# Attention on one core: softmax sums on GpSimd, an image's norms on ScalarE, the first maxima from full-precision operands, filler matmuls, transposed maxima two slots later

## The reference

```python
x = _group_norm(input, gn_weight, gn_bias)                  # 16 groups of 8 channels
qkv = jnp.einsum('bchw,oc->bohw', x, qkv_weight)            # 4 heads of 32 channels: q, k, v
attn = jnp.einsum('bnchw,bncyx->bnhwyx', q, k) / math.sqrt(C)
attn = jax.nn.softmax(attn.reshape(B, N_HEAD, H, W, H * W), axis=-1)      # over 1024 keys
out = jnp.einsum('bnhwyx,bncyx->bnchw', attn, v).reshape(B, C, H, W)
x = jnp.einsum('bchw,oc->bohw', out, out_weight) + out_bias[:, None, None] + input
t = tokens(x)                                               # (B, 1024, 128)
t = t + linear_attention(_ln_t(t))                          # _ln_t: layer norm over the 128 channels
t = t + experts(_ln_t(t))                                   # its own norm, router, top 2 of 8 experts
```

## Time and profile before

| | us |
|---|---|
| median of 3 runs (391.53, 394.69, 396.52) | 394.69 |
| the profiled execution | 393.55 |
| its span in the profile | 391.8 |

### The profile page before, as it was taken

How to read it: one execution, slowest core, us unless ns; L and a number is a source line. 1 busy time by engine, 2 the same in 40 slices (tenths; PEclk the granted TensorE clock), 3 DMA queues, 4 the chain that set the end, 5 groups by cost and what they waited for, 6 DMA issues and landing times.

```text
span 391.8 us, 6547 instructions
## 1 busy us (share of the span) xinstructions
PE 326.7 (83%) x1970; PEld 208.4 (53%) x1970; DVE 222.2 (57%) x693; ACT 187.9 (48%) x272; POOL 112.0 (29%) x142
## 2 busy tenths in 40 slices
PE   1766739998989989999999878198865998999985
PEld 1433323333433433544524254197865998999985
DVE  2446823456464556264655865376978566888610
...
DMA packets 21773, 29.29 MB, mean 75 GB/s; under 512 B 4055, under 2 KB 15628, under 8 KB 21484
## 3 DMA queue, kind: packets, MB, share of 16 engines
...
## 4 chain that ended last, share of the span: by engine, by line
PE 57%; DVE 18%; DMA 7%; POOL 7%; issue 6%; SPq 2%; ACT 1%; ACTq 0%; DVEq 0%; POOLq 0%
PE ps L794 13%; PE ps L989 8%; PE ps L977 8%; PE ps L757 6%; POOL expert_in L473 6%; PE ps L775 5%; DVE above L1081 4%; PE ps L737 3%; DMA Qs<-mrow 2%; SPq L331 2%; DMA Qs<-q_hi 2%; DVE pm L1084 2%; DMA attn<-in_L_conv_qkv_weight 1%; PE ps L859 1%; PE ps L693 1%
## 5 line engine op out<-in xcount | busy, mean ns | idle before, releaser
L536 ACT ACTIVATE probs<-ps 128x1024 f32<-128x1024 f32 x64 | 65.3, 1022 | 43.4 <-PE ps L775 43.4
L794 PE MATMUL ps<-probs,vT 128*32 128x512 f32 x256 | 69.2, 617 | 0.1
L794 PE MATMUL ps<-probs,ones 128*32 128x512 f32 x256 | 69.2, 617 | 0.0
L1081 DVE CUSTOM_DVE_ANT_0 above<-ps,above 128x512 f32<-128x512 f32 x56 | 38.7, 691 | 50.3 <-PE ps L757 49.0
L416 POOL TENSOR_TENSOR rstd<-ve,minus_half 128x8 f32<-128x8 f32 (+1 forms) x8 | 11.1, 1385 | 191.5 <-DVE ve L1120 175.2
L989 PE MATMUL ps<-w,GT 128*128 x368 | 52.8, 289 | 7.9 <-ACT GT L637 7.3
L637 ACT ACTIVATE GT<-H 128x512 f32<-128x512 f32 x46 | 29.0, 631 | 57.4 <-DVE H L1342 57.2
L989 PEld LDWEIGHTS ps<-w,GT 128*128 128x128 f32 x368 | 48.0, 204 | 9.6 <-issue 9.5
L977 PE MATMUL ps<-XTT,w1s 128*128 128x128 f32 x368 | 52.4, 289 | 0.0
L529 ACT ACTIVATE above<-ps 128x512 f32<-128x512 f32 x56 | 33.5, 599 | 38.5 <-PE ps L737 38.5
L478 POOL DMA_INDIRECT token_out<-Y,yidx x46 | 44.1, 959 | 22.1 <-DVE Y L1353 14.3
...
## 6 DMA issues: line engine op xcount, KB each, us to landing
...
```

Of the source, the lines that this page charges most:

```text
L536: nc.scalar.activation(probs[:, s % 3, :], bank(2 + 2 * (s % 2), 2), ACT.Exp).then_inc(exp_done, 1)
L794: last = nc.tensor.matmul(bank(6 + o % 2)[i * HD:(i + 1) * HD, :], w, probs[:, s % 3, hd * HALF:(hd + 1) * HALF], start=kt == 0, stop=kt = ...
L1081: nc.vector.tensor_tensor_reduce(above[:, n % 2, :], bank(base), above[:, n % 2, :], scale=1.0, scalar=-3.0e38, op0=ALU.add, op1=ALU.max, ...
```

## The change

**Sums.** The ones leave `values`. It now has four matmuls of 256 columns: two halves `i` of the 512 queries by two heads, in the four column groups of a bank. POOL adds the probabilities of every four steps (a quad), 128x1024 f32, three adds a quad (one in the last), into one of three buffers (`add_probs`, `quad_sum`). Once in eight steps PE multiplies two such sums with ones (`sums_of`), at the second step of the next output; the last one takes two further tiles of probabilities instead of waiting for their adds. `probs` has five buffers (`probs_of`); an exponential waits for the adds of the step five before. The closing on DVE is one step later.

**Maxima.** The slots of k = 0 are computed by `max_tile` from f32 copies `q32` and `k32` (two more ACT passes) with 32 rows of a head: per query tile four f32 matmuls of 512 columns, two heads by two key halves, in three or four pairs of banks. They stand ahead of image 1's projections, which now wait for those banks, and need no stacks. The transposition of k = 0 stands right behind its eight slots, and ACT issues its DMA; for every other k it stands two slots later than before. The 3 MB of zeros wait for that DMA.

**Norms.** The token norms of image 0 (`F` twice) and the last norm of both images (`X2`) move from DVE to ACT: eight activations of 128x128 each with scale and bias, after DVE has made the shift from mean and factor (`first_shift`, `v_shift`). POOL's powers for image 0 stand between its adds (`NORMS_AT`: after the add of step 35, 50 and 54). The router's logits are taken of the tokens before the norm: the router's weights are centred once ("centre": one matmul and one DVE operation), and `v_gates` multiplies by the norm's factor. So "tokenT" needs `t2` alone. `row_numbers` of image 1 is written after the adds.

**Fillers.** `keep_busy` issues f32 matmuls on the identity into bank 5: 3 at the start, 1 before the weight transposes, 1 of 256 columns and 2 around the group statistics, and 4 ahead of the first transposed maxima.

```diff
+    NPR = 5
+    QUADS = UNITS * 2 * L // P // 4
+    QSPAN = 256
...
+        def probs_of(s):
+            r = s % NPR
+            if r < 3:
+                return probs[:, r, :]
+            return (probs_a if s < UNITS * STEPS // B else probs_b)[:, r - 3, :]
+
+        def quad_sum(q):
+            return (X[:, 1, :], t2[:, 1, :, :].rearrange("p j c -> p (j c)"),
+                    X2[:, 1, :, :].rearrange("p j c -> p (j c)")[:, 0:L])[q % 3]
...
-        order = [(k, i) for k in range(2 * UNITS) for i in range(RING - 1)]
-        for k in range(2 * UNITS):
-            order.insert(min(RING * (k + 1), len(order)), (k, "rows"))
+        order = [(0, QH * hd + t) for t in range(QH) for hd in range(2)]
+        order += [(k, i) for k in range(1, 2 * UNITS) for i in range(RING - 1)]
+        order.insert(PLAIN_FIRST, (0, "rows"))
+        for k in range(1, 2 * UNITS):
+            order.insert(min(RING * (k + 1) + 2, len(order)), (k, "rows"))
...
-            return (6, 7) if g < AHEAD and g % 2 else (0, 1)
+            if g < PLAIN_FIRST:
+                return ((4, 5), (2, 3), (6, 7), (0, 1))[g % 4]
+            return (6, 7) if g == PLAIN_FIRST else (0, 1)
...
-        LAYER1_AT = {BEGIN_LAYER1: "residual", 34: "project", 35: "tokens_stats tokens", 39: "keys",
-                     40: "keys_exp", 41: "query_value0", 42: "query_value1", 44: "keyT", 45: "queries_exp",
+        LAYER1_AT = {BEGIN_LAYER1: "centre residual", 35: "project", 36: "tokens_stats", 38: "tokens", 40: "keys",
+                     41: "keys_exp", 42: "query_value0", 43: "query_value1", 44: "keyT", 45: "queries_exp",
                      46: "queries queries_scaled context", 47: "fold", 48: "queryT", 49: "queryT_sb",
-                     50: "attend stats", 52: "norm stats2", 54: "tokenT", 55: "tokenT_sb", 56: "logits",
-                     57: "gates_exp", 58: "route choose", 60: "counts norm2"}
+                     50: "attend stats", 51: "tokenT", 52: "tokenT_sb norm", 53: "logits",
+                     54: "stats2 gates_exp", 55: "route choose", 56: "shift norm2", 57: "counts"}
         LAYER1_AT_TILE = {"before": "residual project tokens_stats tokens keys keys_exp query_value0 query_value1 "
                                     "keyT queries_exp",
                           0: "queries queries_scaled context", 1: "fold", 2: "queryT queryT_sb", 3: "attend stats",
-                          4: "norm", 5: "stats2 tokenT", 6: "tokenT_sb", 7: "logits", 8: "gates_exp",
-                          9: "route choose counts norm2"}
+                          4: "tokenT tokenT_sb norm", 5: "logits stats2", 6: "gates_exp", 7: "shift route choose norm2",
+                          8: "counts"}
...
-            pool.wait_ge(mhl_ready, 1)
+            pool.wait_ge(mrow_in[0], 16 * 2)
...
+            def add_probs(q, i):
+
+                s = 4 * q + i
+                pool.wait_ge(exp_done, s + 1)
+                if i == 1 and q >= 3:
+                    pool.wait_ge(sum_done, (q - 3) // 2 + 1)
+                if i > 1:
+                    pool.wait_ge(probs_added, added_by(s - 1))
+                nc.gpsimd.tensor_tensor(quad_sum(q), probs_of(s - 1) if i == 1 else quad_sum(q), probs_of(s),
+                                        ALU.add).then_inc(probs_added, 1)
+
+            pool.wait_ge(resid_ready, B)
+            for q in range(QUADS):
+                if q == 1:
+                    pool.wait_ge(xs_zeroed, 16 * B)
+                    row_numbers(0)
+                for i in range(1, 4 if q < QUADS - 1 else 2):
+                    add_probs(q, i)
+                    if (q, i) in NORMS_AT:
+                        rsqrt(B + NORMS_AT[q, i])
...
-                if s >= 3:
-                    act.wait_ge(pv_done, s - 2)
-                nc.scalar.activation(probs[:, s % 3, :], bank(2 + 2 * (s % 2), 2), ACT.Exp).then_inc(exp_done, 1)
+                if s == 3:
+                    act.wait_ge(stack_in[0], 16 * (6 + SP_LOADS))
+                    act.wait_ge(stack_in_pool, 16 * (6 - SP_LOADS))
+                    act.wait_ge(stack_in[1], 16 * 12)
+                if s >= NPR:
+                    act.wait_ge(pv_done, s - NPR + 1)
+                    act.wait_ge(probs_added, added_by(s - NPR))
+                nc.scalar.activation(probs_of(s), bank(2 + 2 * (s % 2), 2), ACT.Exp).then_inc(exp_done, 1)
...
+            def first_apply(i, done):
+
+                act.wait_ge(nm_ready, i + 1)
+                for j in range(J):
+                    last = nc.scalar.activation(F[:, j, :], t2[:, 0, j, :], ACT.Identity, bias=nm[:, i, j:j + 1],
+                                                scale=rstd[:, B + i, j:j + 1])
+                last.then_inc(done, 1)
...
+            act.wait_ge(mrow_ready, 1)
+            for hd in range(2):
+                dst = Qs[SPLIT:STACK, 0, head(0, hd), 0:HALF]
+                act.dma_start(dst.bitcast(f32).rearrange("s (t q) -> s t q", t=QH),
+                              mrow[hd * 2 * QH:(hd + 1) * 2 * QH, :].bitcast(f32)).then_inc(mrow_in[0], 16)
...
+            def keep_busy(n, at_, width=4):
+
+                for i in range(n):
+                    nc.tensor.matmul(bank(at_)[:, 0:width * P], ident[:, :],
+                                     ident[:, :].unsqueeze(1).broadcast_to([P, width, P]), start=True, stop=True)
...
+            def max_tile(t):
+
+                g = 2 * t
+                if t == 0:
+                    pe.wait_ge(hi_ready, 2)
+                    pe.wait_ge(qk_split, 1)
+                    pe.wait_ge(v_sb, 1)
+                elif t == 1:
+                    pe.wait_ge(qk_split, 2)
+                    pe.wait_ge(kd_made, 1)
+                    pe.wait_ge(wT_sb, 2)
+                    pe.wait_ge(vcol_sb, 2)
+                else:
+                    pe.wait_ge(slot_used, g - 2)
+                for h in range(2):
+                    for hd in range(2):
+                        r = slice(HD * head(0, hd), HD * head(0, hd) + HD)
+                        last = nc.tensor.matmul(bank(slot_banks(g + hd)[h]), q32[r, t * P:(t + 1) * P],
+                                                k32[r, h * HALF:(h + 1) * HALF], start=True, stop=True)
+                        if h:
+                            last.then_inc(slot_ready, 1)
...
-            def values(u, step, hd):
-                s = u * STEPS + step
-                b, qh, kt = u // PAIRS, step // KT, step % KT
-                o = 2 * u + qh
-                if hd == 0:
-                    pe.wait_ge(exp_done, s + 1)
-                    if kt == 0:
-                        if o >= 2:
-                            pe.wait_ge(o_used, o - 1)
-                        else:
-                            pe.wait_ge(slot_used, AHEAD)
-                n = head(u, hd)
-                for i, w in ((hd, vT[:, b, kt, n * HD:(n + 1) * HD]), (2 + hd, ones[:, 0:HD])):
-                    last = nc.tensor.matmul(bank(6 + o % 2)[i * HD:(i + 1) * HD, :], w,
-                                            probs[:, s % 3, hd * HALF:(hd + 1) * HALF],
-                                            start=kt == 0, stop=kt == KT - 1)
-                if hd:
-                    last.then_inc(pv_done, 1)
+            def values(s):
+                u, step = s // STEPS, s % STEPS
+                b, kt = u // PAIRS, step % KT
+                o = s // KT
+                pe.wait_ge(exp_done, s + 1)
+                if kt == 0:
+                    if o >= 2:
+                        pe.wait_ge(o_used, o - 1)
+                    else:
+                        pe.wait_ge(slot_used, AHEAD)
+                for i in range(2):
+                    for hd in range(2):
+                        n = head(u, hd)
+                        last = nc.tensor.matmul(query_span(o, i)[hd * HD:(hd + 1) * HD, :],
+                                                vT[:, b, kt, n * HD:(n + 1) * HD],
+                                                probs_of(s)[:, hd * HALF + i * QSPAN:hd * HALF + (i + 1) * QSPAN],
+                                                start=kt == 0, stop=kt == KT - 1)
+                last.then_inc(pv_done, 1)
+
+            def sums_of(o):
+                parts = [quad_sum(2 * o), quad_sum(2 * o + 1)]
+                if o < 2 * UNITS - 1:
+                    pe.wait_ge(probs_added, added_by(KT * o + KT - 1))
+                else:
+                    pe.wait_ge(probs_added, added_by(LAST_QUAD))
+                    parts += [probs_of(LAST_QUAD + 2), probs_of(LAST_QUAD + 3)]
+                if o >= 2:
+                    pe.wait_ge(o_used, o - 1)
+                for n, part in enumerate(parts):
+                    for i in range(2):
+                        for hd in range(2):
+                            r = (2 * i + hd) * HD
+                            last = nc.tensor.matmul(bank(6 + o % 2)[r:r + HD, QSPAN:2 * QSPAN], ones[:, 0:HD],
```

(15 more changed lines are left out.)

159 lines of the change are left out of this document (109 added, 50 removed).

## The result

The changed kernel takes 427.76 us (median of four runs, 425.06 to 428.94) beside 394.38 for the kernel before: a ratio of 1.084, 95% interval 1.0755 to 1.0928. It is slower by 33 us, and the prediction of 383 us, range 367 to 400, is wrong. The profiled execution is the one of 428.94 us, with a span of 427.2.

A forecast was written before the change was run, and what follows sets the result against it. PE, with 57% of the chain, was taken to set the pace. 391.8 - 9.4 + 7.0 + 2.0 + 2.4 - 9.5 - 3.5 = 380.8 us of span, 382.5 with 1.75 outside; adjusted toward the median, 383, range 367 to 400.

The forecast's parts named there:

- The adds: POOL's 128x1024 f32 adds: 2.4 us each, three in four steps, hidden in steps 0 to 31 but not later.
- Values of 256 columns: PE's values in each step: 0.57 us instead of 1.00, giving a two-slot step of 2.58 instead of 2.95.
- the fourth rival: PE's values: halves of 256 columns are held by their eight weight loads, the step is not shortened; 395 us, chance 0.06.
- The stall at step 39: First norm in ACT's queue between exponentials 38 and 39: exponential 39 ends at 9.2, wanted at 5.0, a 4.2 us PE stall.
- The start: Up to the first values: max_tile needs no stacks, first values at 51 instead of 60.5 us; -9.5, between -5 and -12.
- What the adds do to DVE: Steps 0 to 31: 14 DVE operations (L1090, L1091) meet POOL's adds and wait 0.5 us each, +7.0.
- They hinder each other fully: Rival: DVE operations wait for whole adds, 33.6 instead of 7.0, so 410 us; chance 0.16 for over 396.
- Values and sums on PE: Steps 0 to 31: shorter values save 12.1 us, three sums_of give back 2.7, so -9.4.
- Steps 32 to 63: Waits for ACT and POOL: closing 1.0, first norm 4.2, second norm 2.9; +2.0 for the stretch, +2.4 for two shifts.
- half a wait for each shift: Steps 32 to 63: two shifts on DVE, just as POOL starts its next add, wait half an add each, +2.4.
- POOL's pace: Steps 32 to 63: 22 adds and three powers, 57.8 us; last add 3 us after the last values, 77.9 against 75.85, +2.0.
- Behind step 63: After the last values: image 1's norm X2 leaves DVE and its scatter starts earlier; -3.5, from 0 to -6.

The follow-up runs named there:

- kernel 10: The changed kernel with POOL waiting for DVE's mhl and shift operations ahead of nine of its adds, all adds still made: 406.11 us (ratio 1.028).
- Kernel 1: The changed kernel without POOL's adds and the exponentials' waits for them, sums_of taken of a constant: 390.88 us (ratio 0.986).
- kernel 3: The changed kernel without adds and sums_of, with the 512-column values and ones back on PE: 394.29 us (ratio 0.9955).
- The square: Four kernels, ones on PE or PE relieved, without and with adds: 394.3 and 413.9 us with ones, 390.9 and 427.8 relieved.
- kernel 8: The changed kernel with the scores matmuls of steps 32 to 63 issued twice: 425.81 us (ratio 1.075).
- kernel 9: The changed kernel with the scores matmuls of steps 0 to 31 issued twice: 423.75 us (ratio 1.068).
- kernel 2: The changed kernel with the 512-column values and ones back on PE, no sums_of, POOL's adds kept but unused: 413.86 us (ratio 1.050).
- kernel 5: The changed kernel without adds, with ones back on PE and image 0's two norms into F back on DVE: 388.51 us (ratio 0.984).
- kernel 11: The changed kernel without adds, ones on PE, image 0's norms on DVE, parts at the earlier kernel's steps, shift ahead of the route: 384.17 us (ratio 0.974).
- kernel 4: The changed kernel with image 0's two norms into F applied by DVE again, in the same places: 431.5 us (ratio 1.095).

## Why the prediction was wrong

The span came out 46.4 us over the sum: 2.3 at the start, 18.6 in steps 0 to 31, 23.6 in steps 32 to 63, and 1.9 behind.

**What held.** The adds: 2.4 us taken, 2.37 measured. Values of 256 columns: 0.57 us and a two-slot step of 2.58, 102.20 less 99.62 in kernel 10, wherever the clock is full. So the fourth rival falls. The stall at step 39 exists and has the forecast links. The fillers at nothing, and the start's order. One sign did not come: the last add was to end after the last values, and ended at 261.9 us, ahead of them (262.4).

**The start.** -7.3 for -9.5, inside its bounds. With ones and fillers varied, the first values stood at 53.2 to 54.4 in eleven of the twelve kernels.

**"What the adds do to DVE", 7.0.** The waits' own size was not far off: 10.4 us, 0.74 each, where I had 0.8 for a random arrival and took 0.5. What failed is the step from there to time. I let each wait cost its length, at most. Kernel 10 shows that 8.2 us of waits cost 12 to 18, since in the changed kernel PE works at its lower level for long, fully busy (65 to 85 us: busy 20.00 of 20.00, clock 0.50). "They hinder each other fully" was the rival with the right sign and the right places, the route's small operations among them. But in steps 0 to 31 five operations of 14 waited, not all, and the clock did the rest.

**"Values and sums on PE", -9.4.** This was worked out with matmuls at full clock, for which the earlier trace rows (0.95 and 1.00) gave good reason for the kernel before. That the clock could answer the change had no term. Kernel 1 against kernel 3 puts the relief in steps 0 to 31 at -2.4 even with no adds, at a clock of 0.86 against 0.97. Three quarters of the gain are missing; the clock is what differs, though one execution of each is all there is. (Three `sums_of` at the 0.95 of the text are 2.85, not 2.7.)

Both of these steps share an omission: **the granted clock was carried over from the trace of before as if it were a constant**. The range took it in at the start alone, where PEclk was 0.75 already. The square and kernels 8 and 9 say it without a step model: with 19 us of PE work added in kernel 2 the time went down by 14, and 15 us added in kernels 8 and 9 did not lengthen it.

**Steps 32 to 63, +4.4.** Kernel 1, without adds, has +10.9 there: the placing and the norms on ACT. I had priced these waits at 1.0, 4.2 and 2.9. At step 39 the extra over a plain step of 1.23 is 5.0 us without adds and 7.1 in the changed kernel; at step 53 it is 5.1 and 7.3. The eight activations take 3.2 us, not 2.4, and PE comes back at half clock. In the kernels with the ones, 3, 5 and 11, 5.4 us belong to the norms on ACT, 2.4 to the places, and 2.1 are left.

The adds take another 17.1 us. The forecast had two terms for them, half a wait for each shift (+2.4) and POOL's pace, with an end set by the last add. The second failed: no exponential of this stretch waits for POOL, and the last add ends ahead of the last values. The first was too small and too short. Both shifts waited for almost the whole of an add, since the power whose result they need has the next add right behind it in POOL's queue; and seven more operations of DVE waited. Step by step against kernel 1, the changed kernel loses 4.2 us at steps 39 and 53, where the shifts waited 4.3; 5.0 at steps 46 to 48, behind the two long operations of the linear attention, which waited 3.4; and 4.5 at step 57, where the three operations of its chain waited 4.5. The last 3.3 are spread over steps at a lower clock.

Kernel 10 bears this out. With the two shifts free, steps 39 and 53 are as long as without adds (6.12 and 6.38 us, 6.20 and 6.36 in kernel 1), while step 57 is at 7.76 still. The 10.9 us by which its stretch is longer than kernel 1's stand beside 12.8 us of waits in eight other operations of DVE. The 6.2 us between kernel 10 and the changed kernel are less clear: 4.3 are at steps 39 and 53, 2.8 at step 33, and those kernel 9 gained as well, with its shifts waiting. No run frees the route or the attention of their waits, so what these cost is read from the chain and from the steps, not from an experiment.

**Behind step 63, -3.5.** Measured -1.6 for the span. The scatter of image 1 begins 3.6 us earlier in relation to image 1's out projection (336.19 less 267.36, against the earlier trace rows less 230.40), and PE does not use all of that.

**The chances.** Slower by over 2% had 0.11, all of it in one rival that needed random meetings to go badly. The clock would have been a rival of its own, and one that needs no bad luck: in kernel 1, with no adds, it fell to 0.86 all the same.

What stays open: what sets the moments at which the clock falls and comes back. In the changed kernel PE was busy without a pause from 70 to 80 us and stayed at 0.50; in kernel 10 a stretch with some idle time had 1.00. The level in steps 0 to 31 also differed between executions of kernels that were alike up to step 31 (0.72, 0.75, 0.79 in the changed kernel and kernels 8 and 4).
